# Delta stage: row sums from ScalarE's accumulator, and query-key scores one slot later

## What is computed

```python
q = _l2norm(_short_conv_silu(h @ Wq, conv_q_w).reshape(B, T, H, dk)) * scale
k = _l2norm(_short_conv_silu(h @ Wk, conv_k_w).reshape(B, T, H, dk))
v = _short_conv_silu(h @ Wv, conv_v_w).reshape(B, T, H, dv)
def step(S, inp):
    q_t, k_t, v_t, g_t, b_t = inp
    S = S * jnp.exp(g_t)[..., None, None]
    v_old = jnp.einsum('bhk,bhkv->bhv', k_t, S)
    delta = (v_t - v_old) * b_t[..., None]
    S = S + jnp.einsum('bhk,bhv->bhkv', k_t, delta)
    return (S, jnp.einsum('bhk,bhkv->bhv', q_t, S))
_, o = jax.lax.scan(step, S0, xs)
o = _rmsnorm(o, onorm_w) * jax.nn.silu(h @ Wg)
x = x + o @ Wo
```

## Time and profile before

| | |
|---|---|
| time before, median of 3 | 3792.14 us |
| the profiled execution's own time | 3798.17 us |
| its span, first to last instruction | 3795.2 us |
| the delta stage in it | some 1,550 us, of which the 14 full units take 91.6 or 96.1 us each |
| TensorE busy in the span | 3294.0 us, 87% |
| VectorE | 2723.1 us, 72% |
| ScalarE | 2038.1 us, 54% |
| GpSimd | 1804.8 us, 48% |
| granted TensorE clock, mean | 0.951 of full speed |

### The profile page before, as it was taken

One profiled execution on the slowest core, in us unless ns is written; L12 is line 12 of the kernel. 1 busy time (PEld: TensorE's weight loads), 2 busy tenths in 40 slices (PEclk: granted clock), 3 DMA queues, 4 the chain that ended last, 5 costly groups with the idle time before them and its releaser, 6 DMA issues. The chain is left out here.

```text
span 3795.2 us, 87218 instructions
## 1 busy us (share of the span) xinstructions
PE 3294.0 (87%) x32714; PEld 2466.9 (65%) x32714; DVE 2723.1 (72%) x5753; ACT 2038.1 (54%) x4599; POOL 1804.8 (48%) x1647
## 2 busy tenths in 40 slices
PE   4789999999999999968999999986898599899998
PEld 3577777777777777745666566654666366656665
DVE  5577777777777777647777677775999477767775
ACT  3456565656565656513666366632444366636662
POOL 3355555555555555434666166632122466526662
PEclk8689999999999999989999999997999799999999
DMA  4111111111111111033122321222112222131122
GB/s 123 23 24 25 25 25 25 26 25 26 24 27 24 27 25 24 11 95 81 43 53 56 93 50 44 71 79 55 47 50 55 63 49 64 45 95 44 46 71 70
DMA packets 409630, 182.71 MB, mean 48 GB/s; under 512 B 235808, under 2 KB 384384, under 8 KB 406656
## 3 DMA queue, kind: packets, MB, share of 16 engines
q1 hardware_dynamic: 409216, 177.15, 19.0%
HBM read 94.47 MB, written 40.12 MB: 35 GB/s over the span
## 5 line engine op out<-in xcount | busy, mean ns | idle before, releaser
L1197 POOL TENSOR_TENSOR delta_cv<-delta_cv,delta_last_tap 96x256 f32<-96x256 f32 (+1 forms) x384 | 332.7, 867 | 623.4 <-DVE delta_cv L1631 623.4
L1938 POOL TENSOR_TENSOR g_a_rn<-g_a_clip,g_minus_half 128x16 f32<-128x16 f32 x64 | 186.4, 2912 | 271.2 <-DVE g_a_clip L2202 243.0
L1938 POOL TENSOR_TENSOR f_a_rn<-f_a_clip,f_minus_half 128x16 f32<-128x16 f32 x64 | 186.3, 2911 | 260.7 <-DVE f_a_clip L2202 232.5
L2155 ACT ACTIVATE g_a_pr<-g_ps,g_a_nb,g_a_rn 128x128 f32<-128x128 f32 x512 | 185.5, 468 | 146.4 <-DVE g_a_nb L2236 146.4
L2155 ACT ACTIVATE f_a_pr<-f_ps,f_a_nb,f_a_rn 128x128 f32<-128x128 f32 x512 | 185.5, 468 | 146.4 <-DVE f_a_nb L2236 146.4
L1466 ACT ACTIVATE delta_cv<-delta_ps,delta_conv_qk 96x256 f32<-96x256 f32 x256 | 120.9, 472 | 253.5 <-PE delta_ps L1299 252.7
L1623 DVE SCALAR_TENSOR_TENSOR delta_cv<-delta_ps,delta_conv_qk,delta_cv 96x256 f32<-96x256 f32 x256 | 122.1, 477 | 169.5 <-ACT delta_last_tap L1468 169.2
L1243 PE MATMUL delta_ps<-delta_state,delta_qk 96*128 96x192 f32 x1024 | 199.4, 339 | 27.3 <-issue 22.8
L1623 DVE SCALAR_TENSOR_TENSOR delta_cv<-delta_ps,delta_conv_v,delta_cv 128x256 f32<-128x256 f32 x192 | 92.1, 480 | 155.5 <-ACT delta_last_tap L1468 154.1
L1243 PEld LDWEIGHTS delta_ps<-delta_state,delta_qk 96*128 96x128 f32 x1024 | 168.3, 193 | 41.7 <-issue 38.1
L1466 ACT ACTIVATE delta_cv<-delta_ps,delta_conv_v 128x256 f32<-128x256 f32 x192 | 90.5, 471 | 127.5 <-PE delta_ps L1299 127.5
(11 more groups left out here) (350 smaller groups left out, 10477.3 us busy)
## 6 DMA issues: line engine op xcount, KB each, us to landing
f_a_vm<-f_a_v SPq DMA_DIRECT2D x128, 130.0 KB, 2.3
g_a_vm<-g_a_v SPq DMA_DIRECT2D x128, 130.0 KB, 2.3
delta_gd<-delta_dram_row SPq DMA_DIRECT2D x16, 1024.0 KB, 4.6
window_vm<-window_v SPq DMA_DIRECT2D x64, 128.0 KB, 2.3
f_m_x<-y SPq DMA_DIRECT2D x24, 256.0 KB, 3.5
delta_dram_inv<-delta_sub SPq DMA_DIRECT2D x16, 256.0 KB, 2.1
f_m_more<-x SPq DMA_DIRECT2D x16, 256.0 KB, 3.9
x<-f_m_x SPq DMA_DIRECT2D x16, 256.0 KB, 2.3
```

What stands on the lines that cost most here:

```text
L1197: pool.tensor_tensor(cv[0:M, t % 3], cv[0:M, t % 3], last_tap[0:M, t % 3], ALU.add).then_inc(summed.sem, 1)
L1938: pool.tensor_tensor(rn[:, u % 2], clip[:, u % 2], minus_half[:], ALU.pow).then_inc(rn_sb.sem, 1)
L2155: e = act.activation(pr[:, u % 2, half, i, :], ps[:, score_bank(u, half), i * P:(i + 1) * P], ACT.Exp, bias=nb[:, u % 2, half, i:i + 1], s ...
```

## The change

- ScalarE squares each head alone (4 ACTIVATEs of 192 columns in place of one of 768) and writes each one's row sum from its accumulator to `ostat[:, 0, h]`. Before the first it also waits for GpSimd's power of the chunk before (`of_sb`), since `ostat` has one buffer.
- VectorE's four `tensor_reduce` per unit (L1607) go. The eps step waits for the squares in their place. The mark `ostat_step`, 3 per chunk, becomes `ostat_sb`, 1 per chunk; the copies into `vr` (L1512) wait for the squares of three chunks back in place of the sums.
- `KQ_AT` for the second half of the heads goes from slots (17, 18) to (18, 19): TensorE's matmuls, VectorE's product with the decays, and SyncE's load of the next decays (slot 19 to 20) all move with it.

```diff
--- before.py
+++ after.py
@@ -951,7 +951,7 @@
     up_ps = mark("up_ps", 2)
     state_sb = mark("state_sb", 2)
     osq_sb = mark("osq_sb", 2)
-    ostat_step = mark("ostat_step", 3)
+    ostat_sb = mark("ostat_sb")
     of_sb = mark("of_sb")
     o_gated = mark("o_gated", 2)
     o_normed = mark("o_normed", 2)
@@ -986,7 +986,7 @@
 
     K_NORM = 15
     SOLVE_AT = 16
-    KK_AT, KQ_AT = ((6, 7), (9, 10)), ((13, 14), (17, 18))
+    KK_AT, KQ_AT = ((6, 7), (9, 10)), ((13, 14), (18, 19))
     INVERT_AT = dict(x4=23, y4=25, x5=28, y5=30, x6=32, y6=34)
     GATE_AT, OT_AT, Y_AT = (2, 2, 5), (21, 22, 25), 27
 
@@ -1221,7 +1221,7 @@
                         pool.tensor_tensor(mine, mine, gate[:, HB * i * DV:HB * (i + 1) * DV], ALU.mult).then_inc(o_gated.sem, 1)
                 C = chunk(t, 12)
                 if C is not None:
-                    ostat_step.need(pool, C)
+                    ostat_sb.need(pool, C)
                     o_normed.need(pool, C - 1)
                     pool.tensor_tensor(of[:], ostat[:, 1, :], minus_half[:, 0:H], ALU.pow).then_inc(of_sb.sem, 1)
                 for i in range(2):
@@ -1447,8 +1447,10 @@
                 if C is not None:
                     o_sb.need(act, C, i + 1)
                     up_ps.need(act, C, i + 1)
-                    mine = slice(HB * i, HB * i + HB)
-                    act.activation(vr[:, C % 3, mine], o[:, C % 2, mine], ACT.Square).then_inc(osq_sb.sem, 1)
+                    of_sb.need(act, C - 1)
+                    for h in heads(i):
+                        e = act.activation(vr[:, C % 3, h, :], o[:, C % 2, h, :], ACT.Square, accum_out=ostat[:, 0, h:h + 1])
+                    e.then_inc(osq_sb.sem, 1)
                 C = chunk(t, i - 1)
                 if C is not None:
                     q_turned.need(act, C, i + 1)
@@ -1505,7 +1507,7 @@
                         if n is not None:
                             C = 2 * n + cc
                             bvr_sb.need(act, n)
-                            ostat_step.need(act, C - 3, 2)
+                            osq_sb.need(act, C - 3)
                             bank = take(act, ("vt", n, cc, m))
                             for j in range(2):
                                 h = 2 * m + j
@@ -1596,22 +1598,16 @@
                 C = chunk(t, 3)
                 if C is not None:
                     q_summed.need(dve, C)
-                    ostat_step.need(dve, C - 2)
+                    ostat_sb.need(dve, C - 2)
                     dve.tensor_scalar(q_eps[:, C % 2], q_sum[:, C % 2], 1e-6 * DK, 1e-12 * DK, ALU.mult, ALU.add)\
                         .then_inc(q_eps_sb.sem, 1)
-                for i in range(2):
-                    C = chunk(t, 11 + i)
-                    if C is not None:
-                        osq_sb.need(dve, C, i + 1)
-                        mine = slice(HB * i, HB * i + HB)
-                        dve.tensor_reduce(ostat[:, 0, mine], vr[:, C % 3, mine], AX.X, ALU.add).then_inc(ostat_step.sem, 1)
                 C = chunk(t, 12)
                 if C is not None:
                     of_sb.need(dve, C - 1)
-                    ostat_step.need(dve, C, 2)
+                    osq_sb.need(dve, C)
                     q_eps_sb.need(dve, C)
                     dve.scalar_tensor_tensor(out=ostat[:, 1, :], in0=ostat[:, 0, :], scalar=1.0 / DV, in1=q_eps[:, C % 2],
-                                             op0=ALU.mult, op1=ALU.add).then_inc(ostat_step.sem, 1)
+                                             op0=ALU.mult, op1=ALU.add).then_inc(ostat_sb.sem, 1)
 
             def taps(t):
                 n, k = tile_of(t)
```

## The result

Five executions of the changed kernel have a median of 3810.5 us (3805.8 to 3812.0); five of the kernel before, 3787.2 us. The ratio, taken over all ten, is **1.005, 95% interval 1.0039 to 1.0061** (the two medians alone would give 1.006): slower by half a per cent, where the prediction had no difference. Twelve further executions, taken later beside 27 of the kernel before, gave 1.0009 (0.9993 to 1.0025), which is not clear of no difference. The profiled execution took 3807.1 us, 8.9 more than that of before (3798.2).

What follows compares the result with a forecast made beforehand. It took GpSimd's chain to bound slots 16 to 22 and TensorE most others, with clock falls setting unit lengths. Squares +6.3, falls -8.9 and +1.8 gave -0.8; 3798.2 - 0.8 - 6.0 = 3791.4 us, range 3764 to 3818.

Steps and rivals of the forecast that it cites:

- What bounds the kernel: Delta stage: GpSimd's chain sets slots 16 to 22, TensorE mostly follows itself elsewhere; units of 96.08 and 91.64 us alternate by clock.
- VectorE's sums: Slots 17, 18, 3 and 4: removing 60.0 us of sums cannot shorten GpSimd's chain or TensorE's waits; taken as 0.
- The squares: ScalarE, slots 16, 17, 2 and 3: 0.9 us more a group, uncovered only in slot 3 of 7 short units; +6.3 us.
- The check on the low end: ScalarE's squares: by the skill page's ACTIVATE price, four take an estimated 1.1 us, making the term about 2 us.
- The kq products: Second half's score matmuls and VectorE products, one slot later: none added, TensorE still waits until the same 601.88; taken as 0.
- The falls of the clock: TensorE's half clock in slots 3 to 5: 5 long units taken, two fewer falls, -8.9 us, and +1.8 for squares.
- The slower rival: Slot 3's copy: longer wait before L1408 pulls the clock down in every unit; 3823 us, or 3814 for half-length falls; chance 0.28.
- the falls stop: Slots 3 to 5: shifted units pass the edge, all 14 are short and pay 0.9; 3773.7 us, or 3764; chance 0.27.

Runs made afterwards that it cites:

- the best version: Changed kernel with the second half's square moved behind ScalarE's copies in slot 3 alone, against the kernel before: 0.9946, and 0.9943 when run once more.
- the pad in slot 3: Kernel before plus one ACTIVATE squaring 576 columns into an unread buffer, ahead of the second half's square in slot 3 alone: 0.9981.

## Why the prediction was wrong

**What bounds the kernel: right.** In the kernel before and in the changed one the units' lengths follow the clock in slots 3 to 6, and slots 16 to 22 follow GpSimd's chain (16.39 us against 16.33). The second place of a fall was in no row of the kernel before.

**VectorE's sums, 0: right for the chain, open for the whole.** 60.0 us of sums went (VectorE's busy time fell by 53.4) and slots 16 to 22 did not get shorter. But with that work given back the changed kernel was at 1.0041 beside 1.0009 on the same chip, so it can weigh in which arrangement the kernel settles into, and the prediction had no term for that. With the square late in slot 3 and the old slots of the scores it made no difference on one chip (0.9989 with it, 0.9991 without).

**The squares: the mechanism right, the size too high.** +0.65 us a group, where 0.9 was taken between bounds of 0.2 and 1.35. The check on the low end, an estimated 1.1 us for four squares without a read, agrees with the 1.12 us measured. Three of four places were covered as said: the accumulator everywhere but slot 3 gave 0.9985. The uncovered one is slot 3, and the wait for the copy grew by the same 0.65.

**The kq products, 0: right for the kernel before** (0.9995) **and for this change's bound.** In the best version they do not look neutral (0.9943 and 0.9946 against 0.9991, on different chips), and why is open.

**The falls of the clock: the step that failed.** It said that the strict turns of long and short units are "a balance which 0.9 us in every short unit will upset", and so it was; but it went on "I take 5: two fewer falls, -8.9". In the profiled execution nearly all units fell: 11 of 13, not 5 of 14. As a check after the fact, by the step's own working with the measured sizes, if every unit falls: a short unit pays 0.65 and a fall of 3.2, +3.9; a long one loses a little, 96.08 to 95.55, -0.5. Seven of each give +27 - 4 = +23 us, and 3787.2 + 23 = 3810, near the median of the first five executions. Only one of the five was profiled, and there two units did not fall, so that the two agree is in part luck. The step had no ground for its sign: the rows showed that the balance was near an edge, not to which side the kernel would fall.

**The slower rival had the place and the mechanism.** It named L1408's wait in slot 3, half a microsecond as the point from which it decides, and 3814 us for falls of half the length. Only its rule was too simple: a wait of 0.71 to 0.81 us stands in kernels that mostly keep full clock there and in kernels that mostly lose it, and in one of these, with the accumulator in slot 3 alone, six falls of eleven came late in the unit instead. The rival "the falls stop" is as real: 92.2 us a unit in the profiled execution with the pad in slot 3, and 3770 to 3782 us in eight of its twelve. The Trainium skill says that short idle times between groups of matmuls, when they are frequent, can make TensorE's clock fall and rise again and again (TensorE: Matmul & The Clock Gate, A second HAM failure mode: psum-queue depth-cycling; the section that the prediction names is on longer waits, for DMA). The trace agrees that half clock comes back unit after unit (0.50 in 724.60 to 731.40 and in ten other units); that a gap of this size brings it each time, no run here bears out.

**What stays open.** Why the accumulator form settles mostly in the long kind while a pad, 0.07 to 0.10 us shorter by the wait, settles mostly in the short one: the units differ by some hundredths of a microsecond in length and by the reads on ScalarE, and no run separates the two (a pad that gives 0.81 us of waiting would have). What brings the late falls was not tested. Why the changed kernel gave 1.005 once and 1.0009 later is open too. The changed kernel with the square late in slot 3 was faster both times, on two chips; which of the sums and the later scores its gain needs is not settled.

## What to carry to other kernels

When a kernel's repeating unit comes in two lengths that take turns, with the clock as the only difference, it stands at an edge: a change of half a microsecond a unit can go either way by about twice its size, and these rows gave neither its sign nor its size. Several executions are then needed, since the profiled one may be of the rarer kind. Look for falls in the whole unit, not only where the change lies. Then look for the engine work that stands ahead of what TensorE waits for in that place and put it behind: the changed kernel was 0.1% (not clear of no difference) to 0.5% slower with the squares ahead of the copy and, with the copy first, 0.5% faster than the kernel before; the order alone, in the kernel before, gave 0.1% at most. And price an accumulator by its own instruction, not by the ACTIVATE alone.

## What was not expected of the hardware

- Summing along with an ACTIVATE adds a second instruction, ACTIVATION_READ_ACCUMULATOR, 0.193 us each, partly beside the next ACTIVATE's start: four ACTIVATEs of 192 columns took 1.12 us without the sum and 1.49 with it, so a read costs 0.09 us net here.
- The same program with the same waits runs with or without a fall of the clock, in different units of one execution (0.81 us of waiting, 1.11 and 1.94 us for the same 16 matmuls) and, by the times, in different executions (3772.6 us with no fall there, against a median of 3806.7 for its twelve).
- A fall costs by what TensorE has to do in it: 3.2 to 4.4 us a unit in slots 3 to 6, 3.2 behind the second gate product, and up to some 0.4 (92.13 against 91.71) for 6.8 us at the end of GpSimd's chain.
- Units without a fall take 92.2 us with 0.74 or 0.81 us of waiting ahead of x6 and 92.0 to 92.2 with none in brackets: the wait itself shows in the time far less than the falls do.
